# Expert 1's last turn moved to the attention's PSUM bank, behind expert 2's mix, in a one-core attention + four-expert kernel

## The chip, the cores and the metric

One core of one Trainium2 chip runs the whole kernel. The metric is the device time of one execution in microseconds (us); lower is better.

## The reference, cut to what matters

```python
def reference(x, ...):                       # x is (16, 512, 128): 16 groups of 512 tokens of 128
    xn = layernorm(x)
    # attention, without a softmax: scores weighted by decay ** (distance - 1) above the diagonal
    queries, keys, values = xn @ q_w, xn @ k_w, xn @ v_w           # 32 wide
    retrieved = ((queries @ keys.T) * decay_weights) @ values
    att = retrieved @ o_w.T * out_scale
    # routing: the two largest of four logits, softmax over them
    rw, sel = top_k(xn @ router_w + router_b + load_balancer, 2)
    e0 = silu(xn @ sw_w1) * (xn @ sw_w3) @ sw_w2                    # 512 hidden
    e1 = gelu(((xn @ eq + b) @ wv + b) @ wo + b) @ c1w + b) @ c2w + c2b   # 256 hidden
    syn = xn @ ce_syn_w + b
    h2 = layernorm(syn + ((syn @ ce_wv + b) @ ce_wo + b)) * n1g + n1b
    u  = h2 + relu(h2 @ ce_f1w + b) @ ce_f2w + f2b                  # 256 hidden
    e2 = (layernorm(u) * n2g + n2b) @ ce_gen_w + ce_gen_b
    e3 = gelu(xn @ ml_w1 + ml_b1) @ ml_w2 + ml_b2                   # 512 hidden
    return x + att + sum of rw * (the selected two of e0, e1, e2, e3)
```

## The kernel before

The 16 groups are worked off one after another, one **turn** each; the turns 2 to 13 stand in a hardware loop of two turns per pass. Nothing schedules the work: each engine has its own instruction list, written out by hand, and waits on semaphores. A large product is done as three matmuls in reduced precision, high by high, high by low and low by high; the "low" parts are made by subtractions on VectorE (DVE) and GpSimd (POOL).

**TensorE (PE)** in a turn: four products `tok0` to `tok3` of the group's tokens (L1321 to L1323), `gates(0)` (the products a0 and b0, L1308 to L1310, of expert 0's first quarter), four transposes of queries and keys into the bank `ATT` (L1334), `c0` to `c3` of expert 3, `gates(1)`, the attention's scores, then expert 1's product of the group before (L1249 to L1253, into the bank `EX0`) and expert 2's (L1262, into `EX1`), the attention, expert 2's f1 and f2, `gates(2)`, `gates(3)`, expert 3's product, f2 (L1413 to L1415), m0 and m1 for expert 1, and at the end `expert0` (L1229), 16 matmuls in the program (32 in the trace) into `EX0`.

All products named as units (tok0 ... m1, 24 a turn) go round four PSUM banks `S[0..3]`. So a0 lies in the bank of tok0, b0 in that of tok1, c0 and c1 in those of tok2 and tok3. A bank is free when its semaphore `released[b]` has been raised by the engine that read it. For tok0 to tok3 that is DVE, with `pl[t] = tok + bias` (L1039), which waits in turn for ScalarE's (ACT's) copy `kv[t]` (L697).

**Expert outputs.** DVE adds the four experts to `OUT` one after the other, scaled by the routing coefficients. Experts 1 and 3 come out transposed. ACT lays expert 1's product aside as `e1T` (L771, semaphore `e1_laid`), SP's queue writes it to memory and reads it back in four pieces as `e1b`, with 32x32 blocks swapped, and DVE turns the blocks (STREAM_TRANSPOSE, L941) into a PSUM bank and then mixes from there (L945, four instructions, semaphore `ex_taken[1]`). Expert 3 goes the same way (`e3b`, L973, then L918). In the kernel before expert 1 is turned into `EX0`, the same bank that PE's `expert0` writes next. So `expert0` of this turn waits for `ex_taken[1]` of the group before.

**DVE** at the end of a turn: `silu(3)` (L1011, L1019), `sum_expert1` of the group before (L941, L945), `turn_next` (the next group's tokens are turned into the bank `TR`, L988), `expert2` of the group before (L929), `u` (L1108, needs f2 from PE), `x_low` of the next group (L869, needs `xh`), `sum_expert3` of the group before (L973, L918). The next turn begins with the four `pl` (L1039). `x_low` lets PE start the next turn's tok0.

**ACT** before `xh` (L644): eight passes over the tokens `X` of the group after next (`x_moments`, L778 and L782), once their load has landed, and then the copy `xh` from `TR`. SP's queue issues that load (L375) between the two halves of `e1b`'s pieces. **POOL** makes `coef_r` for expert 2's mix (L625).

Of the kernel before, what the change touches and what calls it, by code (L numbers as in the profile page):

```python
# [70 lines left out]
EX_BANK = {0: 0, 1: 0, 2: 1, 3: 1}  # L71
# [57 lines left out]
def wait(eng, sem, value):  # L129
    if not isinstance(value, int) or value > 0:  # L130
        eng.wait_ge(sem, value)


def build(nc: bass.Bass, x: bass.AP, weights: bass.AP, vecs: bass.AP, rows: bass.AP, out: bass.AP):
    with ExitStack() as ctx:
# [35 lines left out]
        OUT = [sb(f"OUT{k}", [P, NT, P]) for k in range(2)]  # L171
# [64 lines left out]
        EX = [ctx.enter_context(nc.psum_tensor(f"EX{b}", [P, NT, P], F32)) for b in range(2)]  # L236
        ATT = ctx.enter_context(nc.psum_tensor("ATT", [P, NT, P], F32))
# [62 lines left out]
        att_added = sem("att_added")  # L300
# [5 lines left out]
        ex_taken = [sem(f"ex_taken{e}") for e in range(E)]  # L306
# [8 lines left out]
        e1_laid = sem("e1_laid")  # L315
# [474 lines left out]
        def _(dve):  # L790
# [34 lines left out]
            n = 1  # L825
# [84 lines left out]
            def mix(g, e, added, bank=None, ready=None):  # L910

                if ready is None:
                    dve.wait_ge(ex_ready[e], g.count(1, 1))
                else:
                    dve.wait_ge(ready, 1)
                dve.wait_ge(added, g.count(1, 1))
                for t in range(NT):
                    ins = dve.scalar_tensor_tensor(out=OUT[g.par][:, t, :], in0=EX[EX_BANK[e] if bank is None else bank][:, t, :],  # L918
                                                   scalar=coef[g.par][:, t, e:e + 1], in1=OUT[g.par][:, t, :],
                                                   op0=ALU.mult, op1=ALU.add)  # L920
                ins.then_inc(ex_taken[e], 1)

            def expert2(g):

                dve.wait_ge(u_scaled, g.count(1, 1))
                dve.wait_ge(ex_ready[2], g.count(1, 1))
                dve.wait_ge(ex_taken[1], g.count(1, 1))
                for t in range(NT):
                    ins = dve.scalar_tensor_tensor(out=OUT[g.par][:, t, :], in0=EX[EX_BANK[2]][:, t, :],  # L929
                                                   scalar=coef_r[:, t:t + 1], in1=OUT[g.par][:, t, :],  # L930
                                                   op0=ALU.mult, op1=ALU.add)
                ins.then_inc(ex_taken[2], 1)
# [1 line left out]
            def expert0(g):  # L934
                mix(g, 0, biases_added)

            def sum_expert1(g):

                dve.wait_ge(e1_swapped, g.count(SWAPS * DMA_INC, SWAPS * DMA_INC))
                dve.wait_ge(ex_taken[0], g.count(1, 1))  # L940
                dve.transpose(EX[EX_BANK[1]][:, :, :].rearrange("p t n -> p (t n)"),  # L941
                              e1b[:, :, :].rearrange("p t n -> p (t n)")).then_inc(e1_turned, 1)
                dve.wait_ge(e1_turned, g.count(1, 1))
                for t in range(NT):
                    ins = dve.scalar_tensor_tensor(out=OUT[g.par][:, t, :], in0=EX[EX_BANK[1]][:, t, :],  # L945
                                                   scalar=coef[g.par][:, t, 1:2], in1=OUT[g.par][:, t, :],
                                                   op0=ALU.mult, op1=ALU.add)
                ins.then_inc(ex_taken[1], 1)
# [20 lines left out]
            def sum_expert3(g):  # L969

                dve.wait_ge(e3_swapped, g.count(SWAPS * DMA_INC, SWAPS * DMA_INC))
                dve.wait_ge(ex_taken[2], g.count(1, 1))
                dve.transpose(EX[EX_BANK[3]][:, :, :].rearrange("p t n -> p (t n)"),  # L973
                              e3b[:, :, :].rearrange("p t n -> p (t n)")).then_inc(ex_ready[3], 1)
                mix(g, 3, ex_taken[2])

            def u_combine(g):
                dve.drain()
# [11 lines left out]
            def turn(g, first, last):  # L990
# [55 lines left out]
                for t in range(NT):  # L1046
                    ins = dve.bn_aggr(mv["c"][:, t, :], stats["c"][:, t, :])
# [50 lines left out]
                if first:  # L1098
                    fold_last()
                silu(3)  # L1100
                if not first:
                    sum_expert1(g.prev())
                if not last:
                    turn_next(g)
                if not first and not last:
                    expert2(g.prev())
                f2, free = unit("f2")
                dve.scalar_tensor_tensor(out=u[:, :], in0=f2[:, :], scalar=vec("f2b"), in1=h2[:, :],  # L1108
                                         op0=ALU.add, op1=ALU.add).then_inc(free, 1)
                if not last:  # L1110
                    x_low(g.next())
                if last:
                    expert2(g.prev())
                    last_u_moments()
                    u_combine(g)
                if not first:
                    sum_expert3(g.prev())
                if last:
                    mix(g, 3, biases_added, LAST3, last_e3)
# [36 lines left out]
        def _(pe):  # L1156
# [64 lines left out]

            def expert0(g):

                wait(pe, ex_taken[1], g.count(1, 0))
                b = g.bank("b3")
                pe.wait_ge(released[b], g.uses_before("b3") + 1)
                for t in range(NT):
                    for j in range(4):
                        ins = pe.matmul(EX[EX_BANK[0]][:, t, :], hid[0][:, j, t * P:(t + 1) * P],  # L1229
                                        scaled[:, j * P:(j + 1) * P], start=(j == 0), stop=(j == 3))  # L1230
                ins.then_inc(ex_ready[0], 1)

            def expert3(g):

                pe.wait_ge(ex_taken[1], g.prev().count(1, 1))
                b = g.bank("e3")
                pe.wait_ge(released[b], g.uses_before("e3") + 1)
                for t in range(NT):
                    ins = pe.transpose(EX[LAST3][:, t, :], e3T[:, t, :], ident[:, :])
                ins.then_inc(last_e3, 1)  # L1240
# [15 lines left out]
            def expert2(g):  # L1256

                wait(pe, ex_taken[3], g.count(1, 0))
                b = g.bank("f2")
                pe.wait_ge(released[b], g.uses_before("f2") + 1)  # L1260
                for t in range(NT):
                    ins = pe.matmul(EX[EX_BANK[2]][:, t, :], u[:, t * P:(t + 1) * P], gen_c[:, :],  # L1262
                                    start=True, stop=True)
                ins.then_inc(ex_ready[2], 1)
# [33 lines left out]
            def turn(g, first, last):  # L1298
# [30 lines left out]
                gates(0)  # L1329
                if not first:  # L1330
                    pe.wait_ge(att_added, g.prev().count(1, 1))
                for t in range(NT):
                    pe.wait_ge(kv_taken, g.count(NT, t + 1))
                    ins = pe.transpose(qk_bank[:, t * P:(t + 1) * P],  # L1334
                                       kv[:, t, 0:2, :, :].rearrange("p a b c -> p (a b c)"), ident[:, :])
# [7 lines left out]
                for n in range(BEHIND):  # L1343
                    ins = pe.matmul(bank[n * C:(n + 1) * C, 0:C], kd[:, n, :], kv[:, n + 1, 2, 0, :],
                                    start=True, stop=True)
# [152 lines left out]
```

## Time and profile before

| | |
|---|---|
| time, median of 3 runs | 441.12 us (438.62 to 441.87) |
| the profiled execution | 438.38 us, of which span 436.6 us |
| granted TensorE clock | 1.00 over the whole span |
| PE busy (matmul) | 423.8 us, 97% of the span |
| DVE busy | 382.2 us, 88% |
| ACT busy | 338.6 us, 78% |
| POOL busy | 330.4 us, 76% |
| DMA | 42.91 MB, mean 98 GB/s |

The span runs from the first to the last instruction; the rest of the time lies around it. Busy time of PE counts matmuls whose ends are modelled and overlap, so starts are the safer thing to read. A row of the timeline has the start and the length in us, engine, line, operation, output and inputs, and in brackets the idle time before it with the one waited for.

### The profile page before, as it was taken

To read this page: it belongs to the slowest core of one execution; us is meant where nothing else is said; L and a number is where in the kernel's file an instruction comes from. 1 tells how busy PE (TensorE), PEld (TensorE's weight loads), DVE (VectorE), ACT (ScalarE), POOL (GpSimd) and SP (SyncE) were. 2 spreads that over 40 slices of the span, in tenths; PEclk is the share of its full clock that TensorE was granted. 3 is DMA by queue.
4 is the path that set the end of the run, shared out by engine and by line. 5 is a ranking of instruction groups with operands and counts; after the bars stand their busy time and mean duration, and the time that the engine had idled before them with its cause. 6 is when DMAs were issued, how large, how long until landed. Compare 5 with 4: busy or idle time off the path is not lost.

```text
span 436.6 us, 9605 instructions
## 1 busy us (share of the span) xinstructions
PE 423.8 (97%) x2610; PEld 355.0 (81%) x2610; DVE 382.2 (88%) x1132; ACT 338.6 (78%) x788; POOL 330.4 (76%) x464
## 2 busy tenths in 40 slices
PE   4989999999999999999999999999999999999996
PEld 4768888887887888788788888888787888878886
DVE  4775999898988989898898998989899898989897
ACT  4977878699786978978798786878978787894860
POOL 3798497795859868696896859779685987857494
PEclk9999999999999999999999999999999999999999
DMA  7522525535353452534435262553535345252321
GB/s 259 48 50 98 94 53 133 111 100 100 92 107 85 120 116 87 109 90 103 95 109 100 92 129 49 137 103 100 98 90 113 79 126 114 97 99 74 72 50 49
DMA packets 154307, 42.91 MB, mean 98 GB/s; under 512 B 128976, under 2 KB 146096, under 8 KB 154288
## 3 DMA queue, kind: packets, MB, share of 16 engines
q1 hardware_dynamic: 154000, 42.67, 42.3%
q8 instruction: 8, 0.13, 0.1%
q14 instruction: 11, 0.09, 0.1%
q10 hardware_dynamic: 288, 0.01, 0.0%
HBM read 22.53 MB, written 19.92 MB: 97 GB/s over the span
## 4 chain that ended last, share of the span: by engine, by line
PE 69%; POOL 8%; DVE 6%; issue 5%; POOLq 4%; DMA 3%; SPq 2%; ACT 2%; DVEq 0%
PE S L1308 11%; PE EX L1229 10%; PE S L1310 10%; PE S L1309 10%; POOL hid3l L563 3%; PE S L1407 2%; PE S L1403 2%; PE S L1402 2%; SPq L407 2%; PE EX L1262 2%; PE S L1323 1%; PE S L1322 1%; PE S L1321 1%; PE TR L1350 1%; PE ATT L1334 1%
## 5 line engine op out<-in xcount | busy, mean ns | idle before, releaser
L563 POOL TENSOR_TENSOR hid3l<-hid,hid3h 128x512 fp32r<-128x512 f32 x64 | 81.0, 1299 | 63.7 <-ACT hid3h L724 63.7
L1308 PE MATMUL S<-xh,WH 128*128 128x512 f32 x224 | 91.8, 410 | 0.0
L1310 PE MATMUL S<-xh,WL 128*128 128x512 f32 x224 | 88.5, 395 | 0.0
L1309 PE MATMUL S<-xl,WH 128*128 128x512 f32 x224 | 88.2, 394 | 0.0
L1229 PEld LDWEIGHTS EX<-scaled,hid 128*128 128x128 f32 x480 | 55.3, 192 | 3.5 <-DVE OUT L945 2.8
L1229 PE MATMUL EX<-scaled,hid 128*128 128x128 f32 x480 | 56.6, 276 | 0.3 <-DVE OUT L945 0.3
L1310 PEld LDWEIGHTS S<-xh,WL 128*128 128x128 f32 x224 | 42.1, 188 | 10.1
L1019 DVE TENSOR_TENSOR hid<-gate,S 128x512 f32<-128x512 f32 x64 | 44.0, 688 | 6.0 <-DVE half L1096 2.5
L1308 PEld LDWEIGHTS S<-xh,WH 128*128 128x128 f32 x224 | 42.1, 188 | 8.4
L1309 PEld LDWEIGHTS S<-xl,WH 128*128 128x128 f32 x224 | 42.4, 189 | 7.9
L1011 DVE SCALAR_TENSOR_TENSOR gate<-th,S 128x512 f32<-128x512 f32 x64 | 43.3, 677 | 0.8 <-ACT th L690 0.2
L690 ACT ACTIVATE th<-S 128x512 f32<-128x512 f32 x64 | 38.3, 598 | 4.7 <-PE S L1310 4.7
L567 POOL TENSOR_TENSOR hidl<-hid,hidh 128x512 fp32r<-128x512 f32 x32 | 40.8, 1296 | 0.5 <-ACT hidh L748 0.5
L711 ACT ACTIVATE hid<-S,VEC 128x512 f32<-128x512 f32 x64 | 38.8, 690 | 0.4
L579 POOL TENSOR_TENSOR hid1l<-hid,hid1h 128x1024 fp32r<-128x1024 f32 x15 | 36.3, 2421 | 2.0 <-ACT hid1h L764 2.0
L778 ACT ACTIVATE xsq<-X 128x128 f32<-128x128 f32 x56 | 16.7, 299 | 26.1 <-DMA X<-x 26.1
L724 ACT CAST hid3h<-hid 128x512 fp32r<-128x512 f32 x64 | 36.3, 621 | 0.0
L918 DVE SCALAR_TENSOR_TENSOR OUT<-EX,coef,OUT 128x128 f32<-128x128 f32 x124 | 34.9, 345 | 1.0
L521 POOL TENSOR_SCALAR n<-pl,negmean_c,rstd_c 128x128 f32<-128x128 f32 x64 | 27.7, 448 | 2.8 <-issue 2.8
L521 POOL TENSOR_SCALAR xn<-X,negmean_x,rstd_x 128x128 f32<-128x128 f32 x60 | 26.5, 456 | 2.6 <-issue 2.6
L1403 PE MATMUL S<-hid3h,WL 128*128 128x512 f32 x64 | 25.3, 395 | 0.0
L1402 PE MATMUL S<-hid3h,WH 128*128 128x512 f32 x64 | 25.2, 394 | 0.0
(218 smaller groups left out, 1132.1 us busy)
## 6 DMA issues: line engine op xcount, KB each, us to landing
X<-x SPq DMA_DIRECT2D x16, 256.0 KB, 3.5
turning<-xn SPq DMA_DIRECT2D x15, 256.0 KB, 2.1
xb<-turning SPq DMA_DIRECT2D x60, 64.0 KB, 2.6
turning<-e3T SPq DMA_DIRECT2D x15, 256.0 KB, 2.0
turning<-u SPq DMA_DIRECT2D x15, 256.0 KB, 2.3
ub<-turning SPq DMA_DIRECT2D x60, 64.0 KB, 2.6
e3b<-turning SPq DMA_DIRECT2D x60, 64.0 KB, 2.7
turning<-e1T SPq DMA_DIRECT2D x15, 256.0 KB, 2.5
```

Of the source, the lines that this page charges most:

```text
L521: pool.tensor_scalar(dst[:, t, :], src[:, t, 0:P], negmean[k][:, t:t + 1], rstd[k][:, t:t + 1], ALU.add, ALU.mult).then_inc(done, 1)
L563: pool.tensor_tensor(hid3l[:, j, :], hid[3][:, j, :], hid3h[:, j, :], ALU.subtract) \
L567: pool.tensor_tensor(hidl[:, j, :], hid[2][:, j, :], hidh[:, j, :], ALU.subtract) \
L579: pool.tensor_tensor(hid1l[:, :, :], hid[1][:, :, :], hid1h[:, :, :], ALU.subtract) \
L690: act.activation(th[:, j, :], a[:, :], ACT.Tanh, scale=0.5).then_inc(th_ready, 1)
L711: act.activation(hid[3][:, j, :], c[:, :], ACT.Gelu, bias=vec(f"ml_b1{j}")).then_inc(free, 1)
L1011: dve.scalar_tensor_tensor(out=gate[:, j, :], in0=th[:, j, :], scalar=1.0, in1=a[:, :], op0=ALU.add, op1=ALU.mult).then_inc(a_free, 1)
L1019: dve.tensor_tensor(hid[0][:, j, :], gate[:, j, :], b[:, :], ALU.mult).then_inc(b_free, 1)
L1229: ins = pe.matmul(EX[EX_BANK[0]][:, t, :], hid[0][:, j, t * P:(t + 1) * P], scaled[:, j * P:(j + 1) * P], start=(j == 0), stop=(j == 3))
L1308: pe.matmul(bank[:, :], wh, hi, start=True, stop=False)
L1309: pe.matmul(bank[:, :], wh, lo, start=False, stop=False)
L1310: pe.matmul(bank[:, :], wl, hi, start=False, stop=True).then_inc(unit_ready, 1)
```

## The change

It has four parts. In all turns but the last, `sum_expert1` turns expert 1 into `ATT` and not into `EX0`; it waits there until the attention of the running turn has been added (`att_added`), and PE's transposes into `ATT` (L1334) wait for `ex_taken[1]`. In the last turn it uses expert 2's bank `EX1`. PE's `expert0` waits for `e1_laid`, ACT's copy, and no longer for DVE's mix. In DVE's list `sum_expert1` stands behind `expert2` and `x_low`, ahead of `sum_expert3`, and `u` stands ahead of `expert2`. The semaphores of the mixes follow the new order 0, 2, 1, 3. No instruction is added or taken away on any engine but register and wait operations.

```diff
@@ DVE, expert2
-                dve.wait_ge(ex_taken[1], g.count(1, 1))
+                dve.wait_ge(ex_taken[0], g.count(1, 1))
@@ DVE
-            def sum_expert1(g):
+            def sum_expert1(g, last):
                 dve.wait_ge(e1_swapped, g.count(SWAPS * DMA_INC, SWAPS * DMA_INC))
-                dve.wait_ge(ex_taken[0], g.count(1, 1))
-                dve.transpose(EX[EX_BANK[1]][:, :, :].rearrange("p t n -> p (t n)"),
+                if last:
+                    way = EX[EX_BANK[2]]
+                    dve.wait_ge(ex_taken[2], g.count(1, 1))
+                else:
+                    way = ATT
+                    dve.wait_ge(att_added, g.next().count(1, 1))
+                dve.transpose(way[:, :, :].rearrange("p t n -> p (t n)"),
                               e1b[:, :, :].rearrange("p t n -> p (t n)")).then_inc(e1_turned, 1)
                 dve.wait_ge(e1_turned, g.count(1, 1))
+                dve.wait_ge(ex_taken[2], g.count(1, 1))
...
@@ DVE, sum_expert3
-                dve.wait_ge(ex_taken[2], g.count(1, 1))
+                dve.wait_ge(ex_taken[1], g.count(1, 1))
@@ DVE, turn
                 silu(3)
-                if not first:
-                    sum_expert1(g.prev())
                 if not last:
                     turn_next(g)
-                if not first and not last:
-                    expert2(g.prev())
                 f2, free = unit("f2")
                 dve.scalar_tensor_tensor(out=u[:, :], in0=f2[:, :], scalar=vec("f2b"), in1=h2[:, :],
                                          op0=ALU.add, op1=ALU.add).then_inc(free, 1)
+                if not first and not last:
+                    expert2(g.prev())
                 if not last:
                     x_low(g.next())
...
                 if not first:
+                    sum_expert1(g.prev(), last)
                     sum_expert3(g.prev())
@@ PE, expert0
-                wait(pe, ex_taken[1], g.count(1, 0))
+                wait(pe, e1_laid, g.count(1, 0))
@@ PE, expert3 (last turn alone)
-                pe.wait_ge(ex_taken[1], g.prev().count(1, 1))
+                pe.wait_ge(e1_laid, g.prev().count(1, 1))
@@ PE, turn, ahead of the transposes of queries and keys
                     pe.wait_ge(att_added, g.prev().count(1, 1))
+                    wait(pe, ex_taken[1], g.prev().prev().count(1, 1))
```

DVE's list from `silu(3)` of a turn in the loop to the next turn's first `pl`, before:

```order
L1019 TENSOR_TENSOR hid<-gate,S 128x512 [waits released2,unit_ready]
L941 STREAM_TRANSPOSE EX<-e1b 128x512 [waits ex_taken0,e1_swapped]
L945 SCALAR_TENSOR_TENSOR OUT<-EX,coef,OUT 128x128 [waits e1_turned]
L945 SCALAR_TENSOR_TENSOR OUT<-EX,coef,OUT 128x128 x3
...
L988 STREAM_TRANSPOSE TR<-xb 128x512 [waits x_swapped]
L929 SCALAR_TENSOR_TENSOR OUT<-EX,coef_r,OUT 128x128 [waits ex_taken1,ex_ready2,u_scaled]
...
L1108 SCALAR_TENSOR_TENSOR u<-S,VEC,h 128x512 [waits unit_ready]
...
L869 TENSOR_TENSOR xl<-TR,xh 128x512 [waits x_high]
L973 STREAM_TRANSPOSE EX<-e3b 128x512 [waits ex_taken2,e3_swapped]
```

The same place in the changed kernel (its lines are numbered a few higher: L946 and L951 are the old L941 and L945, L994 is L988, L1110 is L1108, L979 is L973):

```order
L1025 TENSOR_TENSOR hid<-gate,S 128x512 [waits released2,unit_ready]
...
L994 STREAM_TRANSPOSE TR<-xb 128x512 [waits x_swapped]
...
L1110 SCALAR_TENSOR_TENSOR u<-S,VEC,h 128x512 [waits unit_ready]
L929 SCALAR_TENSOR_TENSOR OUT<-EX,coef_r,OUT 128x128 [waits ex_taken0,ex_ready2,u_scaled]
...
L869 TENSOR_TENSOR xl<-TR,xh 128x512 [waits x_high]
L946 STREAM_TRANSPOSE ATT<-e1b 128x512 [waits att_added,e1_swapped]
L951 SCALAR_TENSOR_TENSOR OUT<-ATT,coef,OUT 128x128 [waits ex_taken2,e1_turned]
L951 SCALAR_TENSOR_TENSOR OUT<-ATT,coef,OUT 128x128 x3
L979 STREAM_TRANSPOSE EX<-e3b 128x512 [waits ex_taken1,e3_swapped]
```

Expert 1's five instructions have gone from the place behind `silu(3)` to the place behind `x_low`, and `u` from behind expert 2 to ahead of it.

PE's list where a turn ends and the next begins, before:

```order
L1229 MATMUL EX<-scaled,hid 128x128 [waits released3,ex_taken1]
...
L131 REGISTER_ALU [waits x_split]
L1321 MATMUL S<-TH,xh 128x228 [waits released0]
...
L1308 MATMUL S<-xh,WH 128x512 [waits released0]
...
L1333 ISA [waits att_added]
L1334 MATMUL ATT<-ident,kv 128x128 [waits kv_taken]
```

and in the changed kernel (L1234 is the old L1229, L1326 is L1321, L1313 is L1308, L1340 is L1334):

```order
L1234 MATMUL EX<-scaled,hid 128x128 [waits released3,e1_laid]
...
L131 REGISTER_ALU [waits x_split]
L1326 MATMUL S<-TH,xh 128x228 [waits released0]
...
L1313 MATMUL S<-xh,WH 128x512 [waits released0]
...
L131 REGISTER_ALU [waits att_added]
L1339 ISA [waits ex_taken1]
L1340 MATMUL ATT<-ident,kv 128x128 [waits kv_taken]
```

No matmul has moved; the wait on `ex_taken1` has gone from `expert0` to the transposes into `ATT`. Both lists have tok0 and then a0 (the L1308 row) waiting for `released0`, which DVE's first `pl` raises for the second of them.

## Rows read from the trace of the kernel before

**Rows 1.** The waits: engine, line, releaser; us in total, times, longest.

```profile
DVE EX L941 <- DMA e1b<-turning: 5.3, 11, 0.9
...
PEld EX L1229 <- DVE OUT L945: 2.8, 7, 0.7
```

**Rows 2.** The timeline of PE (start, length): turns' first tok0, one f2, one a0.

```profile
41.19 0.35 PE L1321 MATMUL S<-TH,xh 128*128 128x228 f32 x1
...
66.91 0.35 PE L1321 MATMUL S<-TH,xh 128*128 128x228 f32 x1
...
217.05 0.40 PE L1415 MATMUL S<-hidh,WL 128*128 128x512 f32 x1
...
222.21 0.35 PE L1321 MATMUL S<-TH,xh 128*128 128x228 f32 x1
...
223.63 0.40 PE L1308 MATMUL S<-xh,WH 128*128 128x512 f32 x1
...
403.08 0.35 PE L1321 MATMUL S<-TH,xh 128*128 128x228 f32 x1
```

**Rows 3.** The timeline of DVE at the end of the same turn.

```profile
216.67 0.73 DVE L941 STREAM_TRANSPOSE EX<-e1b 128x512 f32<-128x512 f32 x1 [0.39 <-DMA e1b<-turning]
...
218.48 0.72 DVE L988 STREAM_TRANSPOSE TR<-xb 128x512 f32<-128x512 f32 x1
219.10 1.08 DVE L929 SCALAR_TENSOR_TENSOR OUT<-EX,coef_r,OUT 128x128 f32<-128x128 f32 x4
220.10 0.74 DVE L1108 SCALAR_TENSOR_TENSOR u<-S,VEC,h 128x512 f32<-128x512 f32 x1
220.76 0.68 DVE L869 TENSOR_TENSOR xl<-TR,xh 128x512 fp32r<-128x512 f32 x1
221.36 0.72 DVE L973 STREAM_TRANSPOSE EX<-e3b 128x512 f32<-128x512 f32 x1
...
223.18 1.30 DVE L1039 TENSOR_TENSOR pl<-S,tokb 128x132 f32<-128x132 f32 x4
```

**Rows 4.** The timeline of ACT, POOL and SP's queue in the same turn.

```profile
216.26 0.31 ACT L778 ACTIVATE xsq<-X 128x128 f32<-128x128 f32 x1 [2.09 <-DMA X<-x]
...
219.23 0.59 ACT L644 CAST xh<-TR 128x512 fp32r<-128x512 f32 x1
...
217.89 0.20 POOL L625 TENSOR_TENSOR coef_r<-coef,rstd_u 128x4 f32<-128x4 f32 x1
...
208.54 0.62 SPq L417 DMA_DIRECT2D turning<-e1T  x1
...
212.50 0.46 SPq L375 DMA_DIRECT2D X<-x  x1
```

**Rows 5.** The timeline of DVE and of PE's weight loads, where expert0 waits longest.

```profile
88.42 1.13 DVE L945 SCALAR_TENSOR_TENSOR OUT<-EX,coef,OUT 128x128 f32<-128x128 f32 x4
...
89.61 3.65 PEld L1229 LDWEIGHTS EX<-scaled,hid 128*128 128x128 f32 x32 [0.73 <-DVE OUT L945]
```

**Rows 6.** The timeline of ACT and PE in the turns with X landing last and first.

```profile
87.34 0.31 ACT L778 ACTIVATE xsq<-X 128x128 f32<-128x128 f32 x1 [2.73 <-DMA X<-x]
...
87.52 0.40 PE L1415 MATMUL S<-hidh,WL 128*128 128x512 f32 x1
...
164.01 0.31 ACT L778 ACTIVATE xsq<-X 128x128 f32<-128x128 f32 x1 [1.31 <-DMA X<-x]
...
165.60 0.40 PE L1415 MATMUL S<-hidh,WL 128*128 128x512 f32 x1
```

**Rows 7.** The timeline of PE and DVE at the end of the last turn.

```profile
423.72 0.40 PE L1415 MATMUL S<-hidh,WL 128*128 128x512 f32 x1
...
424.46 0.74 DVE L1108 SCALAR_TENSOR_TENSOR u<-S,VEC,h 128x512 f32<-128x512 f32 x1
...
427.78 0.69 DVE L973 STREAM_TRANSPOSE EX<-e3b 128x512 f32<-128x512 f32 x1
...
433.89 0.34 DVE L1148 SCALAR_TENSOR_TENSOR OUT<-S,coef,OUT 128x128 f32<-128x128 f32 x1
```

More of the change, by code:

```diff
@@ L935, in expert0 @@
                 mix(g, 0, biases_added)
-            def sum_expert1(g):
+            def sum_expert1(g, last):
                 dve.wait_ge(e1_swapped, g.count(SWAPS * DMA_INC, SWAPS * DMA_INC))
-                dve.wait_ge(ex_taken[0], g.count(1, 1))
-                dve.transpose(EX[EX_BANK[1]][:, :, :].rearrange("p t n -> p (t n)"),
+                if last:
[5 more added lines that the diff above has]
+                dve.transpose(way[:, :, :].rearrange("p t n -> p (t n)"),
                               e1b[:, :, :].rearrange("p t n -> p (t n)")).then_inc(e1_turned, 1)
                 dve.wait_ge(e1_turned, g.count(1, 1))
+                dve.wait_ge(ex_taken[2], g.count(1, 1))
                 for t in range(NT):
-                    ins = dve.scalar_tensor_tensor(out=OUT[g.par][:, t, :], in0=EX[EX_BANK[1]][:, t, :],
+                    ins = dve.scalar_tensor_tensor(out=OUT[g.par][:, t, :], in0=way[:, t, :],
                                                    scalar=coef[g.par][:, t, 1:2], in1=OUT[g.par][:, t, :],
@@ L971, in sum_expert3 @@
                 dve.wait_ge(e3_swapped, g.count(SWAPS * DMA_INC, SWAPS * DMA_INC))
-                dve.wait_ge(ex_taken[2], g.count(1, 1))
+                dve.wait_ge(ex_taken[1], g.count(1, 1))
                 dve.transpose(EX[EX_BANK[3]][:, :, :].rearrange("p t n -> p (t n)"),
                               e3b[:, :, :].rearrange("p t n -> p (t n)")).then_inc(ex_ready[3], 1)
-                mix(g, 3, ex_taken[2])
+                mix(g, 3, ex_taken[1])
             def u_combine(g):
```

## The prediction, made before the changed kernel was timed

> **What bounds the kernel now.** I read the page first, then the waits, then the timelines of all engines over two turns, and last the starts of each turn over the whole span. The granted clock is full everywhere, so starts can be compared across the trace. PE has no long gap. From its first tok0 at 41.19 to the last at 403.08 lie 14 turns in 361.89 us, 25.85 us each; the fastest of them, 41.19 to 66.91, takes 25.72 [rows 2]. A turn in which PE never waits is about that. So 14 x 25.72 = 360.08, and all waits of PE in these 14 turns come to 1.8 us. That is the most that any change of waits can give back there.
>
> Where are those 1.8 us? The waits put down 2.8 us of weight-load idleness in 7 places to `expert0` waiting for DVE's mix of expert 1, the longest 0.7 [rows 1]; the weight load normally runs ahead of its matmul, so this overstates PE's loss. In the worst turn DVE's L945 ends at 88.42 + 1.13 = 89.55 and PE starts 0.06 later, at 89.61 [rows 5]. DVE is late there because it waits for `e1b` (5.3 us in 11 places [rows 1]). The wait that the change takes away is real and small.
>
> What the reader should see next is how little room DVE has. In the turn of rows 2 to 4 it runs from 216.67 to 223.18 without a gap, and the first `pl` (223.18, a quarter of 1.30, so done at about 223.5) is what frees the bank for a0, which PE starts at 223.63; a0's weights are loaded some 0.1 earlier, at 223.53 [rows 2, 3]. With 0.06 us for the semaphore [rows 5] nothing is left. Here a0 comes 1.42 us after tok0 and the first `pl` 0.97, and in all 15 turns behind the first both distances are the same to 0.01. So DVE is never late for a0, but it can't be later either.
>
> **The change part by part.** Durations are start-to-start distances on DVE [rows 3]: `sum_expert1` 1.81, `turn_next` 0.62, `expert2` 1.00, `u` 0.66, `x_low` 0.60, `sum_expert3` 1.82, together 6.51.
>
> *The wait of expert0.* `e1_laid` is raised by ACT ahead of SP's store of e1T, at 208.54 [rows 4], 10 us ahead of `expert0`, so PE no longer waits: -1.8 us over the 14 turns. It can't be more by the count above; if it were only part of that, the lower bound is 0.
>
> *The new order on DVE.* Write F for the end of f2 on PE, 217.05 + 0.40 = 217.45 [rows 2]. `silu(3)` ends at 216.28, where L941's wait begins [rows 3]. Before, the time until F is filled by expert 1 after a wait of 0.39. Now `turn_next` fills 0.62 of it and DVE then stands still until F, because `u` needs f2: u starts at about F + 0.1 = 217.55. Then `expert2` at 218.21; its `coef_r` from POOL is there at 217.89 + 0.20 = 218.09 [rows 4], so it is just in time. `x_low` could start at 219.21. But it needs `xh`, and ACT gets to `xh` at 219.23 after its passes over X, which begin when X lands at 216.26, and ends it at 219.82 [rows 4]. Before, that was hidden, for DVE came to `x_low` only at 220.76. Now `x_low` starts at 219.86, `sum_expert1` at 220.46, `sum_expert3` at 222.27 and the first `pl` at 224.09, against 223.18 before. So what is late next is `pl`, and behind it a0 on PE: by 0.91 us in this turn, and by 219.21 + 4.23 - 223.18 = 0.26 if X had landed early enough. When a0 waits, its first weight load isn't hidden, which I put at 0.1 (it was 0.1 ahead before). PE's loss is 0.36 to 1.01 us a turn.
>
> *What the stall gives back.* A stall at a0 moves PE's later work, but not the chain by POOL and SP that brings X, which starts from work done ahead of a0 (xn of the group after next). SP's queue is full from there to the store of e1T at 208.54, 1.0 us behind ACT's copy, and the X load at 212.50 follows from that [rows 4]. So X lands earlier against PE by the last turn's stall d. The balance is d = 1.01 - d, about 0.5, and never below 0.36. X's landing scatters: against F it comes 0.58 us before in the latest turn (87.34 against 87.92) and 1.99 before in the earliest (164.01 against 166.00) [rows 6]; the mean of the 13 turns that load X is 1.4, that of rows 2 to 4 is 1.19. The mean alone gives d = 0.4; the late ones and the floor raise it. I take 0.5 for each of the 14 turns: +7.0 us. The bounds: 0.3 a turn if half of my weight-load term and a little of the floor is wrong, +4.2; 0.95 if X's chain gives nothing back, +13.3.
>
> *The wait ahead of the transposes into ATT.* DVE's mix of expert 1 now ends before `sum_expert3` begins, at about 222.3, and PE's transposes come two products behind a0, later than 223.63 + 1.4 [rows 2, 3]. It costs nothing; queued behind it are c0 to c3, and it would begin to cost if expert 1 were over 2.5 us later. `att_added` for the turn into ATT is over 5 us old by then.
>
> *The DMAs.* None is issued in another order. `e1b` is read some 4 us later, so DVE's 5.3 us of waiting for it [rows 1] vanish; that is already in the sum, as DVE stands still for F instead. The store of OUT waits for expert 3's mix, some 0.9 later, and SP's queue has the copy of xn ahead of it anyway.
>
> *The last turn.* DVE is the chain here: from `u` at 424.46 to the last mix at 433.89 it has no gap over 0.3 us [rows 7]. Before, expert 1 filled DVE's time before f2 was there (F = 424.12). Now `u` starts at 424.22, 0.24 earlier, of which the transposes of `u` on PE, which follow m1, let through about half, and the 1.81 of expert 1 stand behind it, ahead of L973. So +1.7 us (1.6 to 1.8).
>
> **Sum.** -1.8 + 7.0 + 1.7 = +6.9 us on the profiled execution: 438.4 + 6.9 = 445.3. The profiled run is at the low end of the three runs, whose median is 2.7 higher; the difference should carry over, so I forecast 441.1 + 6.9 = 448.0.
>
> A page rule speaks against this. The Trainium skill (Perfetto Trace Analysis, Optimization Strategy) has one find the gaps on the engine that limits, follow their semaphore, and make that dependency start sooner or complete faster. By it the change gives 1.8 us and no more is to be asked. The trace agrees that this gap exists; it also shows the next dependency with no slack behind it, and by that row the sum turns over.
>
> **Rivals.**
> *The order is absorbed (no change).* For a0 not to stall, DVE would need 0.26 us or more of room at `pl` that my reading misses: if f2's modelled end is late by that much (u starts earlier), or a0's wait is later than its weight load shows. And X would have to land in time, since before it is landing 1.0 us or more too late for `x_low` at 219.21 in most turns. Then -1.8 + 1.7 = -0.1: 441.0. With half of the floor in place, 443. Against it: DVE's starts after a PE release trail the modelled end by about 0.1 everywhere.
> *The wait is all that counts (faster).* The mechanism is the skill's: expert0 freed, the tail covered by PE and POOL instead of DVE. -1.8: 439.3, still within 1%. Over 1% faster needs 4.4 us, more than PE waits in all the turns; it would have to come from runs slower than the profiled one, whose extra 2.7 us could be the same wait. 436.6 at best.
> *X's chain gives nothing back (slower still).* If X's landing follows PE, each turn pays 0.85 to 1.01: +13.3 - 0.1, 454. For it: X waits on `att_added` too; against it, SP's queue is late by itself ahead of the load, by the 1.0 us named above.
>
> **Chances.** The stall at a0 as forecast 0.70, absorbed 0.20, the wait alone 0.04, X's chain 0.06. The likeliest case's own range is 444.5 to 452. A measurement of this kernel tells about 1% (4.4 us) from no change; 445.5 is the line. Of the 0.70 some 0.10 fall under it. So slower by over 1%: 0.60 + 0.06 = 0.66; within 1%: 0.10 + 0.18 + 0.03 = 0.31; faster: 0.03. The range for 8 in 10 is 442.0 to 453.0.
>
> **What would show it.** In the changed profile: no wait of L1234 on DVE; a new wait of PE (or its weight load) at L1313, released by DVE's `pl` (L1045), in 14 turns at 0.4 to 1.0; turns of about 26.2 us; DVE idle before L1110 on PE's f2 by about 0.6 and before L869 on ACT's `xh`; no idle before L946; and the stretch from F to the last mix in the last turn 1.7 us longer. The forecast is wrong if a0 stays 1.42 us behind tok0, or if X's landing moves otherwise than with PE's stall.

## The result and the profile after

The changed kernel takes 448.23 us (446.49 to 448.79, 4 runs) against 441.5 us (438.62 to 442.89, 4 runs) for the kernel before: a ratio of 1.0142 with a 95% interval of 1.0102 to 1.0182. It is slower, by 6.7 us in the medians. (The ratio is an estimate from all the runs of both kernels and so not exactly the quotient of the two medians, 1.0152; this holds for all ratios below.) Two more series of the same kernel gave 1.0166 (1.0135 to 1.0197) and 1.0176 (1.0146 to 1.0206). The profiled execution took 448.07 us with a span of 446.3.

Four rows of the changed kernel's list of waits (us in total, times, longest) answer to [rows 1]:

```profile
DVE u L1110 <- PE S L1421: 10.0, 15, 1.4
PEld S L1313 <- DVE pl L1045: 8.8, 14, 1.8
...
PE S L1313 <- DVE pl L1045: 6.2, 14, 1.6
...
DVE xl L869 <- ACT xh L644: 4.4, 6, 1.4
```

Neither `expert0`'s wait for DVE nor DVE's wait for `e1b` is there any more. In their place a0 (L1313) waits for DVE's `pl` in all 14 turns, DVE waits for f2 (L1421) ahead of `u`, and in six turns it waits for `xh` (before: in two). Rows for a turn in which X lands early, first DVE, then PE (start, length), to be laid beside [rows 2, 3]:

```profile
193.36 0.72 DVE L994 STREAM_TRANSPOSE TR<-xb 128x512 f32<-128x512 f32 x1
194.67 0.75 DVE L1110 SCALAR_TENSOR_TENSOR u<-S,VEC,h 128x512 f32<-128x512 f32 x1 [0.59 <-PE S L1421]
195.34 1.12 DVE L929 SCALAR_TENSOR_TENSOR OUT<-EX,coef_r,OUT 128x128 f32<-128x128 f32 x4
196.37 0.68 DVE L869 TENSOR_TENSOR xl<-TR,xh 128x512 fp32r<-128x512 f32 x1
196.97 0.72 DVE L946 STREAM_TRANSPOSE ATT<-e1b 128x512 f32<-128x512 f32 x1
197.72 1.13 DVE L951 SCALAR_TENSOR_TENSOR OUT<-ATT,coef,OUT 128x128 f32<-128x128 f32 x4
198.96 0.73 DVE L979 STREAM_TRANSPOSE EX<-e3b 128x512 f32<-128x512 f32 x1
...
200.76 0.89 DVE L1045 TENSOR_TENSOR pl<-S,tokb 128x132 f32<-128x132 f32 x4
```

```profile
194.24 0.40 PE L1421 MATMUL S<-hidh,WL 128*128 128x512 f32 x1
...
199.35 0.35 PE L1326 MATMUL S<-TH,xh 128*128 128x228 f32 x1
...
201.10 0.50 PE L1313 MATMUL S<-xh,WH 128*128 128x512 f32 x1 [0.17 <-DVE pl L1045]
201.44 0.39 PE L1314 MATMUL S<-xl,WH 128*128 128x512 f32 x1
```

Tok0 starts at 199.35 and a0 at 201.10, 1.75 later instead of 1.42: a0 is 0.33 late. The next matmul follows 0.34 later and not 0.24 as before, since a0's weight load was not hidden: 0.10 more. In a turn with a late X (DVE, then PE):

```profile
117.83 0.69 DVE L869 TENSOR_TENSOR xl<-TR,xh 128x512 fp32r<-128x512 f32 x1 [1.36 <-ACT xh L644]
```

```profile
119.37 0.35 PE L1326 MATMUL S<-TH,xh 128*128 128x228 f32 x1
...
122.56 0.50 PE L1313 MATMUL S<-xh,WH 128*128 128x512 f32 x1 [1.62 <-DVE pl L1045]
```

Here a0 comes 3.19 us after tok0, 1.77 late. From the first tok0 behind turn 0 to the last one, and from there to the end of the span:

```profile
40.77 0.35 PE L1326 MATMUL S<-TH,xh 128*128 128x228 f32 x1
...
410.67 0.35 PE L1326 MATMUL S<-TH,xh 128*128 128x228 f32 x1
```

| stretch | before | after | difference |
|---|---|---|---|
| start to the tok0 of turn 1 | 41.19 | 40.77 | -0.42 |
| 14 turns | 361.89 | 369.90 | +8.01 |
| last tok0 to the end of the span | 33.52 | 35.63 | +2.11 |
| span | 436.6 | 446.3 | +9.7 |

a0's lateness against 1.42 adds up to 8.40 us over the 14 turns, 0.60 on average and 0.32 at least; with 0.10 for each weight load the stall costs 9.8 us, of which 0.4 falls to the last row of the table. (These are the a0 of the turns 2 to 15, the last one. The a0 of turn 1, ahead of which no expert 1 stands, isn't late here.)

### The profile page after: what moved, and what is told of

It is laid out like the page before. It is cut to its first block, busy times and chain, and to the rows that moved or that the text cites. A ratio compares the mean times of both kernels' runs of the same rounds, so it can differ in the third digit from the quotient of the medians.

```text
span 446.3 us, 9626 instructions
## 1 busy us (share of the span) xinstructions
PE 426.6 (96%) x2610; PEld 356.4 (80%) x2610; DVE 380.4 (85%) x1132; ACT 337.2 (76%) x788; POOL 330.5 (74%) x464
## 4 chain that ended last, share of the span: by engine, by line
POOL 27%; PE 25%; issue 18%; POOLq 15%; DVE 8%; DMA 3%; ACT 2%; SPq 2%; DVEq 0%; ACTq 0%
POOL hid3l L563 10%; POOL hid1l L579 5%; PE S L1313 5%; PE S L1315 4%; PE S L1314 4%; POOLq L587 3%; POOL xn L521 3%; POOL n L521 3%; POOL OUT L600 3%; POOLq L624 2%; POOLq L536 2%; POOL hidl L567 2%; POOLq L599 2%; POOLq L515 2%; SPq L407 2%
## 5 line engine op out<-in xcount | busy, mean ns | idle before, releaser
L1313 PE MATMUL S<-xh,WH 128*128 128x512 f32 x224 | 93.1, 415 | 6.2 <-DVE pl L1045 6.2
L1234 PEld LDWEIGHTS EX<-scaled,hid 128*128 128x128 f32 x480 | 55.9, 192 | 1.3
L1234 PE MATMUL EX<-scaled,hid 128*128 128x128 f32 x480 | 56.0, 275 | 0.0
L1313 PEld LDWEIGHTS S<-xh,WH 128*128 128x128 f32 x224 | 42.1, 188 | 17.2 <-DVE pl L1045 8.8
L697 ACT COPY kv<-S 128x192 f32<-128x192 f32 x64 | 20.1, 320 | 15.4 <-PE S L1328 14.7
L521 POOL TENSOR_SCALAR xn<-X,negmean_x,rstd_x 128x128 f32<-128x128 f32 x60 | 26.5, 456 | 2.6 <-issue 2.6
```

Of the source, the lines that this page charges most:

```text
L521: pool.tensor_scalar(dst[:, t, :], src[:, t, 0:P], negmean[k][:, t:t + 1], rstd[k][:, t:t + 1], ALU.add, ALU.mult).then_inc(done, 1)
L1313: pe.matmul(bank[:, :], wh, hi, start=True, stop=False)
```

## The experiments

Every kernel was run beside the kernel before on the same chip. "a0 late" is the sum of (a0 - tok0 - 1.42) over the turns 2 to 15 of the profiled execution, its weight loads not counted; "rest" is the span behind the last tok0.

| kernel | median us | ratio to before (95%) | 14 turns | a0 late | rest |
|---|---|---|---|---|---|
| before | - | 1 | 361.89 | 0.0 | 33.52 |
| changed | 448.23 | 1.0142 (1.0102 to 1.0182) | 369.90 | 8.4 | 35.63 |
| e1_bank_alone | 440.72 | 0.9996 (0.9973 to 1.0018) | 364.55 | 1.3 | 33.51 |
| e2_u_behind | 453.51 | 1.0301 (1.0260 to 1.0342) | 374.27 | 12.7 | 35.98 |
| e3_split_moments | 447.30 | 1.0136 (1.0109 to 1.0163) | 367.68 | 5.1 | 35.58 |
| e4_next_then_e1 | 439.12 | 0.9960 (0.9937 to 0.9983) | 361.73 | 0.7 | 33.46 |
| after_again | 447.61 | 1.0166 (1.0135 to 1.0197) | 367.83 | 6.1 | 35.66 |
| e3_again | 447.09 | 1.0154 (1.0126 to 1.0181) | 367.03 | 4.8 | 35.58 |
| e5_old_last_turn | 446.39 | 1.0142 (1.0110 to 1.0173) | 369.79 | 6.6 | 33.90 |
| e6_filler | 452.57 | 1.0284 (1.0238 to 1.0329) | 374.19 | - | 35.55 |
| e7_e4_split | 440.11 | 0.9974 (0.9950 to 0.9999) | 363.56 | 0.8 | 33.47 |
| e8_filler_psum | 446.59 | 1.0085 (1.0058 to 1.0113) | 367.50 | 3.4 | 33.54 |
| e9_no_chained_wait | 446.85 | 1.0136 (1.0095 to 1.0176) | 367.47 | 5.6 | 35.42 |
| after_third | 447.76 | 1.0176 (1.0146 to 1.0206) | 368.42 | 6.8 | 35.59 |

### The bank and the wait without the order: e1_bank_alone

```diff
 (kernel before, DVE, sum_expert1, cut)
-                dve.wait_ge(ex_taken[0], g.count(1, 1))
-                dve.transpose(EX[EX_BANK[1]][:, :, :]...
+                dve.wait_ge(att_added, g.next().count(1, 1))
+                dve.transpose(ATT[:, :, :]...
...
 (PE, expert0)
-                wait(pe, ex_taken[1], g.count(1, 0))
+                wait(pe, e1_laid, g.count(1, 0))
 (PE, ahead of the transposes into ATT)
+                    wait(pe, ex_taken[1], g.prev().prev().count(1, 1))
```

> The kernel before with the first two parts of the change alone: expert 1 is turned into ATT, and expert0 waits for e1_laid; DVE's order stays as it was before (expert 1 behind silu(3), u behind expert 2). My theory, that DVE has no room ahead of a0: the time that DVE loses to e1b's landing (5.3 us in 11 places) no longer stops expert0 but comes out again at the first pl and so at a0; PE's waits stay near 1.8 us over the 14 turns, they only change their place; 441.5 us, ratio to before 0.998 to 1.003. Rival, that the wait of expert0 is all that counts: PE's waits vanish and the time falls by 1.8 us, ratio 0.996.

Measured: 0.9996. The sign that tells the two apart is in the trace, DVE first, then PE:

```profile
88.43 0.73 DVE L941 STREAM_TRANSPOSE ATT<-e1b 128x512 f32<-128x512 f32 x1 [1.03 <-DMA e1b<-turning]
```

```profile
93.33 0.37 PE L1322 MATMUL S<-TH,xh 128*128 128x228 f32 x1
...
95.25 0.50 PE L1309 MATMUL S<-xh,WH 128*128 128x512 f32 x1 [0.33 <-DVE pl L1040]
```

`expert0` no longer waits, the same late `e1b` now makes a0 late, 1.92 instead of 1.42 behind tok0. It happens in four of the 14 turns, by 0.06 to 0.50. (The 14 turns of this profile also hold a late a0 in turn 1, 0.86 us, from a late X in turn 0, and 0.8 us of one wait of the attention's product.) So the wait of `expert0` was not a loss that could be taken away by itself: where DVE was late, it was paid at the next thing that DVE releases. The time shows no gain, and the rival's 0.996 lies outside the interval.

### The order: e4_next_then_e1 and e2_u_behind

e4 has the parts of e1 and this order (the last turn as before):

```diff
 (e1_bank_alone, DVE, turn)
-                if not first:
-                    sum_expert1(g.prev())
                 if not last:
                     turn_next(g)
+                if not first:
+                    sum_expert1(g.prev())
-                if not first and not last:
-                    expert2(g.prev())
                 (u)
+                if not first and not last:
+                    expert2(g.prev())
```

> The two parts of e1_bank_alone with a third order on DVE: turn_next, expert 1 (into ATT), u, expert 2, x_low, expert 3; in the last turn expert 1, u, expert 2 as before. My theory: turn_next covers e1b's landing, expert 1 covers the time until f2, and DVE comes to the first pl about 0.3 us ahead of the limit; neither expert0 nor a0 waits, 14 turns of 25.72 us, so 1.8 us less than before, 439.7, ratio 0.996. Rival, that moving work to the end of DVE's turn is what costs, wherever expert 1 stands: 443 or more, ratio above 1.003.

Measured: 0.9960, as the theory had it, 439.12 us, and faster than both kernels of the study. Nine of its 14 turns take 25.72 or 25.73 us. In such a turn DVE has no hole from `silu(3)` to `pl`, and there it is DVE that waits, for ACT:

```profile
189.79 0.72 DVE L989 STREAM_TRANSPOSE TR<-xb 128x512 f32<-128x512 f32 x1
190.42 0.69 DVE L941 STREAM_TRANSPOSE ATT<-e1b 128x512 f32<-128x512 f32 x1
191.14 1.13 DVE L946 SCALAR_TENSOR_TENSOR OUT<-ATT,coef,OUT 128x128 f32<-128x128 f32 x4
192.18 0.74 DVE L1107 SCALAR_TENSOR_TENSOR u<-S,VEC,h 128x512 f32<-128x512 f32 x1
...
196.72 1.30 DVE L1040 TENSOR_TENSOR pl<-S,tokb 128x132 f32<-128x132 f32 x4 [0.38 <-ACT kv L697]
```

`turn_next` covers `e1b`'s landing (in 10 of the 14 turns wholly), expert 1 covers the time until f2. Apart from the last turn, e4 and the changed kernel differ in expert 1's place in DVE's list alone and in the waits that follow from it, so that place is what costs, and not the bank. Two things aren't shown. The gain is in the medians (1.75 us); the 14 turns of the two profiled executions take 361.73 and 361.89 us, nearly the same, since a0 is late by 0.7 in all in e4's. And this order wasn't run with the old bank and the old wait, so how much of the gain needs them stays open.

```diff
 (changed kernel, DVE, turn)
+                if not first and not last:
+                    expert2(g.prev())
                 (u)
-                if not first and not last:
-                    expert2(g.prev())
```

> The changed kernel with u put back behind expert 2, the rest as changed. My theory: DVE stands still behind turn_next anyway; expert 2 then has to wait for POOL's coef_r, which is there 4.13 us ahead of tok0, where u could start 4.69 ahead; so x_low, expert 1 and the first pl come 0.4 later in turns where X doesn't hold x_low, and a0 waits 0.7 or more in every turn instead of 0.32 or more; turns in which X lands late absorb it. 450 to 452 us, ratio 1.020 to 1.024. Rival, that u's place is indifferent because X's landing sets x_low: as the changed kernel, 448.2, ratio 1.014 to 1.016.

Measured: 1.0301, worse than my 1.020 to 1.024, in the direction that I expected. DVE stands still longer, for POOL (DVE, then PE):

```profile
196.94 1.13 DVE L929 SCALAR_TENSOR_TENSOR OUT<-EX,coef_r,OUT 128x128 f32<-128x128 f32 x4 [1.17 <-POOL coef_r L625]
```

```profile
201.04 0.35 PE L1326 MATMUL S<-TH,xh 128*128 128x228 f32 x1
```

and a0 is 0.9 late in most turns, nearly without scatter. What I had short is the distance itself: expert 2 starts 4.10 us ahead of tok0 here, where `u` starts 4.68 ahead in the changed kernel (194.67 and 199.35). That is 0.58 later, as a0's lateness says (0.90 against 0.32), and I had taken 0.4. Having `u` first is the useful part of the change's new order.

### What holds x_low: e3_split_moments, e3_again and e7_e4_split

```diff
 (ACT, turn)
                 if two_more(g):
-                    x_moments(Group(g.pair, g.off + 2))
+                    x_means(Group(g.pair, g.off + 2))
                 if not last:
                     take_x(g.next())
+                if two_more(g):
+                    x_squares(Group(g.pair, g.off + 2))
```

> The changed kernel with ACT's eight passes over X split: the four that sum stay ahead of the copy xh, the four that square come behind it. xh is then ready 1.6 us earlier. My theory, in which X's landing through ACT holds x_low in six or seven of the 14 turns: the long waits of a0 (0.5 to 1.8 us) vanish, all 14 turns wait 0.32 to 0.35 us, and DVE has no wait for xh; 9.8 - 14 x 0.42 = 3.9 us less than the changed kernel, 444.3 us, ratio 1.006. Rival, that the scatter of a0's waits comes from DVE itself or from the DMA traffic: still 447 to 448, ratio 1.013.

> The kernel of e3_split_moments again. Its profile had a0's waits flat as my theory said, but two losses elsewhere (1.1 us in the start, 1.1 in turn 1 behind the landing of ub's pieces). If those are scatter of one execution, this profile's span is 2 us or more shorter than that of after_again and the median of the time 1.5 to 3 us below it; if splitting the moments itself costs them, the losses are there again and the median is within 1 us of the changed kernel's.

In both profiles the mechanism is as expected: from turn 3 on a0 comes 1.74 or 1.75 behind tok0, with one exception of 1.93, and the long waits are gone. The time is another matter: 447.30 and 447.09, only 0.5 to 0.9 us under the changed kernel, where I had expected 3.9 and then 1.5 to 3. One reason is plain: the first profile of the changed kernel had an unusual scatter, a0 late by 8.4 us in all against 6.1 and 6.8 in the two later ones; the floor of 14 x 0.32 = 4.5 is most of it, 0.4 more is a longer wait behind L951 in turn 2 (see e9), and X's part is 1.3 to 3.6 us. On the same chip the 14 turns of e3_again are 0.8 us shorter than those of after_again (367.03 and 367.83), which agrees with the 0.5 in the medians: a0 is 1.3 less late, and the first of the turns is 0.6 longer by a wait for `ub`, the pieces of `u` that come back from memory. Both e3 profiles also lose time at the start, of which more below. That isn't the split's doing, as e7, with the same split, and after_third, without it, show; whether it weighs on the medians isn't known, since the starts of the other executions weren't recorded.

> The kernel of e4_next_then_e1 with ACT's moment passes split round the copy xh as in e3. In e4's profile four of the 14 turns still have a0 0.04 to 0.29 us late, each with X landing late. My theory: they vanish, all 14 turns take 25.72; if PE's first products again run at half pace until about 15.5 us, as in both profiles of the split, the start eats about 1.2 us and the sum is near e4's or 0.5 above it: ratio to before 0.995 to 0.999. If the start is not the split's doing, 1 us less than e4: ratio 0.993 to 0.995.

e7 has a clean start and a ratio of 0.9974. The late a0 of e4's turns in the loop vanish, but `e1b` lands late in the first turns (0.49 and 0.27 of lateness), and a wait for `ub`'s pieces costs 0.8. Its interval and e4's overlap: nothing gained over e4 that can be measured.

### DVE's room, measured by itself: e6_filler and e8_filler_psum

```diff
 (kernel before, DVE, turn, behind sum_expert3 in turns 1 to 14)
+                if not first and not last:
+                    dve.tensor_tensor(filler[:, :], u[:, :], h2[:, :], ALU.add)      # e6
+                    dve.tensor_copy(filler[:, :], TR[:, :])                          # e8
```

> The kernel before with one more DVE operation behind sum_expert3 in the turns 1 to 14, an addition of two 128x512 tiles into a tile that nobody reads (0.6 to 0.7 us). It measures DVE's room ahead of a0 by itself. My theory (room 0 to 0.45 us, by turn, 0.15 on average): a0 waits about 0.5 + 0.1 us a turn, the waits of expert0 (1.8 us in all) shrink since e1b has more time; 446.5 to 448.5, ratio 1.013 to 1.018. Rival, that DVE has room of 0.6 or more and the changed kernel's loss comes from X alone: within 1 us of before, ratio 0.998 to 1.003.

> e6_filler with another operation in the same place: a copy of the bank TR (PSUM) into the tile that nobody reads, one input only and none from SBUF. In e6 the addition of two SBUF tiles took 0.68 us in 12 turns and 2.83 and 2.50 in two, where it began just behind the start of POOL's hid1l. If that is contention for SBUF between DVE and POOL, this copy takes 0.6 to 0.7 in all 14 turns, and DVE's room shows cleanly: a0 waits 0.02 to 0.5 a turn behind it, 445 to 448 us, ratio 1.011 to 1.018. If the long ones are there again, the contention is something else. Rival, that DVE has room of 0.6 or more: ratio 0.998 to 1.003.

e8 is the clean one for this question. Its copy takes 0.68 in all 14 turns (0.60 from its start to the next). In a turn where DVE was just in time before, DVE and PE show

```profile
201.66 0.68 DVE L1120 COPY filler<-TR 128x512 f32<-128x512 f32 x1
202.26 0.89 DVE L1040 TENSOR_TENSOR pl<-S,tokb 128x132 f32<-128x132 f32 x4
```

```profile
202.60 0.50 PE L1311 MATMUL S<-xh,WH 128*128 128x512 f32 x1 [0.30 <-DVE pl L1040]
```

with tok0 at 200.72: the first `pl` starts 1.54 behind tok0 instead of 0.97, 0.57 later for 0.60 put in; a0 is 0.46 late, 0.56 with its weight load. So DVE's room is nothing in these turns. The whole ratio of 1.0085 is under my range of 1.011 to 1.018: in five turns a0 isn't late at all. Four of them follow a turn with a stall of 0.46 or 0.47, and in them DVE doesn't wait for `e1b`: the stall lets it land early against DVE (in three of the four `pl` is still 0.11 late and the weight load not hidden). The rival with room in every turn is out; so is my average of 0.5 a turn for a stall of this kind, which was 0.24, or 0.33 with the weight loads.

The profiled execution of e8 has a loss of another kind: from 26.5 to 33.3 us the granted clock was 0.50, the lower of its two levels, and turn 1's tok0 came at 43.86 instead of 41.19. That lies ahead of the 14 turns. Another of its seven executions has the same mean clock of 0.99 and the other five 0.999 or 1.00, so the median is little touched.

e6 is slower than e8 though its instruction does the same amount of work. Two of its 14 took 2.83 and 2.50 us. The first of them, on DVE, and what POOL did at that time:

```profile
95.11 2.83 DVE L1120 TENSOR_TENSOR filler<-u,h 128x512 f32<-128x512 f32 x1
```

```profile
95.01 2.37 POOL L580 TENSOR_TENSOR hid1l<-hid,hid1h 128x1024 fp32r<-128x1024 f32 x1
```

DVE's addition of two SBUF tiles started 0.1 behind POOL's subtraction of two SBUF tiles, and ended 0.56 after it. In the second, in turn 15, the addition began 0.44 behind the subtraction; e8's copy in turn 15 began 0.44 behind the same subtraction and took 0.68. e6, DVE and POOL, then e8, DVE and POOL:

```profile
415.40 2.50 DVE L1120 TENSOR_TENSOR filler<-u,h 128x512 f32<-128x512 f32 x1
414.96 2.39 POOL L580 TENSOR_TENSOR hid1l<-hid,hid1h 128x1024 fp32r<-128x1024 f32 x1 [2.10 <-ACT hid1h L765]
```

```profile
411.67 0.68 DVE L1120 COPY filler<-TR 128x512 f32<-128x512 f32 x1
411.23 2.42 POOL L580 TENSOR_TENSOR hid1l<-hid,hid1h 128x1024 fp32r<-128x1024 f32 x1 [1.78 <-ACT hid1h L765]
```

Behind the first long one PE stood still for 2.45 us, and from 99.0 to 102.4 the granted clock was 0.50. e6 doesn't measure the room, then, and I don't use its time.

### The last turn: e5_old_last_turn

```diff
 (changed kernel, DVE, turn; expert 1 into ATT in all turns)
                 silu(3)
+                if last:
+                    sum_expert1(g.prev(), last)
...
-                if not first:
+                if not first and not last:
                     sum_expert1(g.prev(), last)
```

> The changed kernel with the last turn as it was before: expert 1 straight behind silu(3), then u, expert 2, expert 3. My theory of the last turn, in which DVE is the chain: the stretch from the last turn's first tok0 to the end of the span is 1.8 us shorter than in the changed kernel (33.8 against 35.6), time 1.7 us less, ratio to before 1.010 to 1.012. Rival, that PE and POOL set the end: no change, 1.015.

The stretch behind the last tok0 is 33.90, against 35.66 in after_again on the same chip and 35.59 to 35.66 in all profiles of the changed kernel: 1.7 to 1.8 us, as expected. The rest of 0.4 above 33.52 is the stall of the last a0. The medians differ by 1.2 us (1.0142 against 1.0166), less than the 1.7 that I expected, with intervals that overlap; the trace settles the term, the time alone wouldn't.

### A wait on the instruction just in front: e9_no_chained_wait

```diff
 (changed kernel, DVE, sum_expert3)
-                dve.wait_ge(ex_taken[1], g.count(1, 1))
+                dve.wait_ge(ex_taken[1 if last else 2], g.count(1, 1))
                 dve.transpose(EX[EX_BANK[3]]...
```

> The changed kernel with one wait loosened: the transposition of expert 3 waits for ex_taken[2] (the last reader of its bank) and no longer for ex_taken[1], which the instruction right in front of it raises; the mix behind it still waits for ex_taken[1]. The last turn stays as changed. In the changed kernel L951 and L979 start 1.24 apart, where L945 and L988 stood 1.04 apart before. My theory, that this 0.2 is the wait on the instruction just in front and is part of a0's 0.32: L951 to L979 falls to 1.04, a0's floor to 0.12 or 0.13, the loss a turn by 0.2, so 2.5 to 2.8 us less than the changed kernel, ratio to before 1.008 to 1.010. Rival, that the 0.2 belongs to the transposition itself and not to the wait: as the changed kernel, 1.014 to 1.017.

> The changed kernel again on the same chip, for e9's sake. Ratio to before 1.013 to 1.018.

```profile
197.60 1.13 DVE L951 SCALAR_TENSOR_TENSOR OUT<-ATT,coef,OUT 128x128 f32<-128x128 f32 x4
198.64 0.72 DVE L979 STREAM_TRANSPOSE EX<-e3b 128x512 f32<-128x512 f32 x1
```

L951 to L979 is 1.04 here and 1.24 in the changed kernel (197.72 to 198.96 above), and the smallest lateness of a0 is 0.12 instead of 0.32. In turn 2 the wait is longer: a0 is 0.68 or 0.69 late there in all three profiles of the changed kernel, and 0.12 here. So at least 0.2 us of a0's lateness is a wait that the order of the mixes doesn't need at that place. The time falls less than by 14 x 0.2: by 0.9 us in the medians, 1.0136 against 1.0176 on the same chip, with intervals that overlap, and my 1.008 to 1.010 was missed. The trace settles the wait; a gain in time isn't shown. The balance in the prediction would explain it: with a smaller stall X lands later against PE. In the profile seven of the 14 turns are 0.33 to 1.16 late where the floor alone would be 0.12.

> The changed kernel once more, as the reference for the three others on this chip. Ratio to before 1.012 to 1.019. In the profile the a0 of the 14 turns waits 0.32 us or more each, with some waits of 0.5 to 1.8 where X lands late, in other turns than last time if that is scatter of the DMAs.

after_again's ratio was within this. Its waits of 0.5 us and more behind a late X lie in the turns 8 and 12, where the first profile has two of its five; in after_third they lie in the turns 4 and 13.

## Why the prediction was right

448.0 was forecast, 448.2 measured. The mechanism is the one forecast; that the number is so close is in part luck, as the terms show.

- **The wait of expert0**: taken away by itself it gave nothing (e1); with an order that keeps DVE in time the median fell by 1.75 us (e4), as large as the term of 1.8, though the two profiled executions don't show it. In the changed kernel the term can't be seen apart from the stall: the forecast took 1.8 off and added the stall, and a0's lateness contains what DVE would have been late for `expert0`.
- **The stall at a0** is there in all 14 turns, released by `pl`, as forecast. The floor was put at 0.36 with its weight load and is 0.42. The term that was mis-sized in it is the distance from `x_low` to `sum_expert3`: I took 0.60 + 1.81, and it is 2.59, for `sum_expert3` now waits on the mix just in front of it (e9). Against that `u` starts 0.03 behind f2's modelled end and not 0.1, so the distance that I took for a rule does not hold in this place.
- **The average of 0.5 a turn** was too low: 9.8 us instead of 7.0 in the first profile, 7.5 in after_again (6.09 + 14 x 0.10), 8.2 in after_third. The cause is the floor, turn 2 and X's scatter. The balance itself shows: in the first profile a0 is 1.77 late in the turn of tok0 119.37, and in the next turn X lands 7.24 us ahead of tok0 instead of 5.01, and a0 is back at the floor.
- **The last turn**: +1.7 forecast, 1.7 to 1.8 by e5, and 0.4 more for its a0, which the forecast counted with the turns.
- **The transposes into ATT** wait for nothing, as said: no row of the changed kernel's waits has PE or its weight load waiting at L1340.
- **The sum against the profiled execution** was +6.9; it was +9.7. The difference of the medians is smaller, 6.7 here and 7.2 or 7.3 in the two later series, for the profiled execution of before was a fast one (438.38 where the medians of five series lie at 440.35 to 441.72) and that of the changed kernel was not. With 7.5 to 8.2 for the stall the sum is 7.4 to 8.1, so the term of the stall was too small, and the terms as the profiles give them are up to 1.4 us more than what the medians show. That these two all but cancel is luck, and where the difference goes stays open.

The rival "the order is absorbed" fell with e8 and the trace; "the wait is all that counts" fell with e1. That X's chain gives nothing back is refuted by the turns that follow a long stall. The Trainium skill's rule (Perfetto Trace Analysis, Optimization Strategy), to make the dependency behind the limiting engine's gap start sooner, agrees with e4 and disagrees with e1 as a forecast: there the gap went away and the time stayed.

## What to carry to other kernels

Before a wait of the limiting engine is removed, look at what else waits for the same late engine, and how much room it has there: here DVE was late, and whether PE paid for it at `expert0` or at a0, the time was the same. When work is moved in an in-order list, place it where the engine would stand still anyway (here until f2), not where it fills nothing; with `sum_expert1` one place further back the kernel was faster than before, with it four places further back slower, and apart from the last turn these two differ in little else. And let a moved instruction wait only for what it needs: a semaphore raised by the instruction just in front cost 0.2 us a turn.

## What the runs showed of the hardware

**Two SBUF inputs on DVE against two on POOL.** In e6 an addition of two 128x512 tiles in SBUF took 0.68 to 0.76 us in 12 turns and 2.83 and 2.50 in the two where it began 0.10 and 0.44 behind POOL's `hid1l`. e8's copy, with its one input in PSUM, took 0.68 in 14 of 14, also where it began 0.44 behind `hid1l`. The long ones ended 0.56 and 0.55 behind POOL's end. It goes the other way too: where e6's addition began first, 0.13 ahead (204.22 and 204.35), it took 0.70 and `hid1l` 2.85 instead of 2.4, and in 11 turns the one of POOL's `xn` (128x128, 0.45 us each beside e8's copy) that began between 0.10 us ahead of the addition and 0.20 behind it took 0.88 to 0.97. Of the addition and `hid1l` the one that began later lost the time.

**PE's pace in the start.** In all 14 profiles the first products, which start between 5.6 and 6.0 us, run at half the pace: their starts, from 7.7 us on, are 0.21 us apart, and later 0.11. In ten profiles the pace changes between 9.4 and 11.3 us, among the idle products; in four (after_third, e3_split_moments, e3_again, e9) only between 15.3 and 15.9, so that tok0 is slow as well. after_third and the changed kernel's first profile, the same program:

```profile
14.10 0.53 PE L1326 MATMUL S<-TH,xh 128*128 128x228 f32 x1 [0.28 <-DVE xl L869]
14.42 0.42 PE L1327 MATMUL S<-TL,xh 128*128 128x228 f32 x1
14.63 0.42 PE L1328 MATMUL S<-TH,xl 128*128 128x228 f32 x1
...
15.83 0.27 PE L1328 MATMUL S<-TH,xl 128*128 128x228 f32 x1
15.94 0.27 PE L1326 MATMUL S<-TH,xh 128*128 128x228 f32 x1
```

```profile
13.17 0.35 PE L1326 MATMUL S<-TH,xh 128*128 128x228 f32 x1 [0.89 <-DVE xl L869]
13.35 0.28 PE L1327 MATMUL S<-TL,xh 128*128 128x228 f32 x1
13.47 0.27 PE L1328 MATMUL S<-TH,xl 128*128 128x228 f32 x1
```

The page gives a granted clock of 1.00 for this stretch in both, and for the kernel before over the whole span. But the trace's own record of the granted clock begins only at 15.71 in after_third, at 10.54 in the changed kernel's first profile and at 11.26 in the kernel before, each at full speed and within 0.05 us of the change of pace; ahead of it there is no record. A factor of two is also what the clock's two levels make where they are recorded: in e8's profile the 128x512 products start 0.43 us apart at a granted clock of 0.50 and 0.23 apart at 1.00. So the slow start is most likely the lower level. Turn 1's tok0 comes at 42.49 instead of 40.77, 1.7 us later; in the other three it comes at 42.19 to 42.64. It is scatter of the execution, not of the kernel, for the same program has it and hasn't. What decides it stays open.
